# One fused kernel's feed-forward stage, reordered: the second product 14 slots behind the first, the token maximum between taps, VectorE's results in PSUM, the second norm's steps spread out

## What is computed

```
h  = layernorm(x1)
h  = bit_linear(h, w1)          # 1024 -> 4096: tokens rounded to 127 levels of their own maximum,
                                #               weights rounded to -1, 0, 1
h  = depthwise_conv1d(h)        # three taps along the sequence, one set for each of 4096 channels
h  = silu(h)
out = x1 + bit_linear(h, w2)    # 4096 -> 1024, tokens rounded to 127 levels of their own maximum
```

## Time and profile before

| what | value |
|---|---|
| runs | 1073.35 us median of three (1069.76 to 1102.9) |
| the profiled execution | 1075.98 us, of which the slowest core's span is 1074.4 us |
| spans of the 8 cores | 1056.5 to 1074.4 us |
| busy share of the span | PE 83%, DVE 75%, ACT 65%, POOL 64% |
| second stage | 522.1 us to the end, 552 us |
| first product of slots 0, 16, 24, 48, 56 begins | 522.1, 634.5, 698.2, 888.7, 947.7 us |
| the last first product ends | 1000.7 us |

### The profile page before, as it was taken

How to read it: one execution, slowest core, us unless ns; L and a number is a source line. 1 busy time by engine, 2 the same in 40 slices (tenths; PEclk the granted TensorE clock), 3 DMA queues, 4 the chain that set the end, 5 groups by cost and what they waited for, 6 DMA issues and landing times.

```text
span 1074.4 us, 23923 instructions; the slowest of 8 cores (1056.5 to 1074.4 us)
## 1 busy us (share of the span) xinstructions
PE 895.0 (83%) x7282; PEld 539.3 (50%) x7340; DVE 806.9 (75%) x1293; ACT 698.2 (65%) x1116; POOL 682.7 (64%) x912
## 2 busy tenths in 40 slices
PE   2999989897957778866676578999989899999898
PEld 1454545454524444433554455666656565666443
DVE  2674776777778888977377979898897989888631
ACT  3553888797827676868686866767677676766200
POOL 2211755646655768565454795959879597979590
PEclk9999999999979999967888989999999999999899
DMA  8910777666665766684744221423314233332112
GB/s 265 328 62 1 197 209 236 244 201 223 206 211 173 217 196 202 211 296 161 261 172 182 71 87 59 158 99 132 125 66 151 99 121 116 116 105 96 40 41 77
DMA packets 38749, 166.89 MB, mean 155 GB/s; under 512 B 4833, under 2 KB 4962, under 8 KB 29922
## 3 DMA queue, kind: packets, MB, share of 16 engines
q1 hardware_dynamic: 34210, 148.59, 41.8%
q0 software_dynamic: 4416, 16.78, 4.4%
HBM read 140.18 MB, written 25.17 MB: 154 GB/s over the span
## 4 chain that ended last, share of the span: by engine, by line
PE 42%; DVE 19%; issue 12%; POOL 9%; ACT 8%; DMA 7%; DVEq 1%; SPq 1%; POOLq 0%; ACTq 0%
PE psM L843 9%; PE psO L861 9%; POOL hs L618 6%; PE psQK L680 6%; PE psV L660 5%; PE psS L738 5%; PE psPV L757 5%; DVE hs L1367 3%; ACT PT L999 3%; DVE t1s L1208 3%; DVE amx L1386 3%; ACT hs L1044 2%; DMA wvst<-wv 2%; DMA t1scr<-t8s 2%; ACT tb L1048 2%
## 5 line engine op out<-in xcount | busy, mean ns | idle before, releaser
L999 ACT ACTIVATE PT<-psS,nbias 128x1024 bf16<-128x1024 f32 (+1 forms) x320 | 297.5, 985 | 89.2 <-PE psS L738 85.5
L843 PE MATMUL psM<-xqT,w1b 128*128 128x258 bf16 x2048 | 249.7, 283 | 44.3 <-DVE hs L1367 35.6
L609 POOL TENSOR_TENSOR hs<-hs,tb 128x256 f32<-128x256 f32 x256 | 200.1, 811 | 106.7 <-DVE hs L1367 106.1
L843 PEld LDWEIGHTS psM<-xqT,w1b 128*128 128x128 fp8e4 x2048 | 203.9, 101 | 91.5 <-issue 54.1
L1044 ACT ACTIVATE hs<-psM,convb_s,convw_s 128x256 f32<-128x256 f32 x256 | 146.3, 572 | 99.5 <-PE psM L843 88.0
L618 POOL TENSOR_TENSOR hs<-hs,srow 128x256 f32<-128x256 f32 x256 | 190.0, 775 | 12.0 <-ACT srow L1062 12.0
L680 PE MATMUL psQK<-ln1T,wqkb 128*128 128x512 bf16 x430 | 116.6, 391 | 23.3 <-DVE qkO L1135 7.4
L757 PE MATMUL psPV<-vaug,PT 128*128 128x65 bf16 x2176 | 116.9, 200 | 19.7 <-DVE ctx L1189 10.7
L757 PEld LDWEIGHTS psPV<-vaug,PT 128*128 128x128 bf16 x2176 | 93.1, 101 | 80.1 <-issue 59.4
L1367 DVE SCALAR_TENSOR_TENSOR hs<-psM,convw_s,hs 128x256 f32<-128x256 f32 x256 | 108.5, 473 | 20.1 <-ACT tb L1048 19.4
L1048 ACT ACTIVATE tb<-psM,convw_s 128x256 f32<-128x256 f32 x256 | 121.7, 475 | 0.0
(11 more groups left out here) (125 smaller groups left out, 1132.8 us busy)
## 6 DMA issues: line engine op xcount, KB each, us to landing
wbuf<-w1q SPq DMA_DIRECT2D x32, 1024.0 KB, 6.4
wbuf<-w2p SPq DMA_DIRECT2D x32, 1024.0 KB, 5.9
w1b<-t1scr SPq DMA_DIRECT2D x64, 512.0 KB, 3.5
x<-x SPq DMA_DIRECT2D x16, 512.0 KB, 15.0
wqkst<-wqk POOLq DMA_DIRECT2D x16, 512.0 KB, 6.7
x1scr<-x POOLq DMA_DIRECT2D x4, 2048.0 KB, 10.1
x1g<-x1scr SPq DMA_DIRECT2D x16, 512.0 KB, 4.4
out<-x1g SPq DMA_DIRECT2D x16, 512.0 KB, 2.6
```

The source lines that it names most:

```text
L609: e.tensor_tensor(hs_quad(q)[:, part], hs_quad(q)[:, part], tb_quad(q)[:, part], ALU.add).then_inc(g_add, 1)
L843: inst = e.matmul(psM[j][:, 0:GRP + 2], w1b[:, at:at + 128], xqT[:, x0:x0 + GRP + 2], start=(kc == 0), stop=(kc == 7))
L999: e.activation(out=pt_unit(u).rearrange("p (h w) -> p h w", w=512)[:, :, 128 * j:512], in_=psS[u % 2][:].rearrange("p (h w) -> p h w", w=512)[
```

## The change

Nothing changes in what is computed. The parts are:

1. **Lag.** The second product runs 14 slots behind the first (`LAG`), so it begins in slot 14 and ends in slot 77. Its eight parts come in another order: the first half of the channels for both output halves, then the second half for both. The tables are moved: quad 3 is scaled in b=3 instead of b=4, quad 7 in b=6 instead of b=7, quad 3 is rounded in b=4 instead of b=5 and quad 7 in b=7 instead of b=0 of the group after.
2. **Maximum between taps.** On DVE `widen_max(q-1)` stands between the taps of tiles 0 and 1 and those of tiles 2 and 3 of slot q; before, it stood behind all four. The rounding stands at the end of a slot.
3. **PSUM.** A bank `psD` holds `amx`, the identity that `token_scale` multiplies, and most of the small columns of the second norm. The bank comes from `psTb` and `psNb`, which now share one; for that `transpose_xq` and `turn_max` wait for each other's readers.
4. **Divided norm.** `stats` becomes `moments2`, `largest` and `smallest`, placed one at a time in slots b=4 to b=7 and b=0; before, both tiles' steps stood in b=0 and b=1. The batch for group 1 moves into the last pair of heads (steps 29, 31 and 36), and `x1t` has four slots. In group 0 rounding and transposes come two slots earlier.
5. **DMA.** The four loads of `w2T` are issued in slots 3 to 6, one each; before, all four in slot 5.

```
-        SCALED = {2: (0, 1), 3: (2,), 4: (3, 4), 5: (5,), 6: (6,), 7: (7,)}
-        ROUNDED = {3: (0, 1), 4: (2,), 5: (3, 4), 6: (5,), 7: (6,)}
+        SCALED = {2: (0, 1), 3: (2, 3), 4: (4,), 5: (5,), 6: (6, 7)}
+        ROUNDED = {3: (0, 1), 4: (2, 3), 5: (4,), 6: (5,), 7: (6, 7)}
+        LAG = 14
...
+        TAKEN = (1, 3)
...
-            def second(g, b):
-                m, n, half = b // 4, (b // 2) % 2, b % 2
+            def second(k):
+                g, i = divmod(k, 8)
+                m, half, n = i // 4, i // 2 % 2, i % 2
...
-                    if G >= 2:
-                        second(G - 2, b)
+                    if LAG <= 8 * G + b < LAG + 8 * NGRP:
+                        second(8 * G + b - LAG)
...
                     e.wait_ge(v_max, q)
-                    done(e.tensor_reduce(amx[:], rows, AX.X, ALU.max,
+                    done(e.tensor_reduce(psD[:, 0:GRP], rows, AX.X, ALU.max,
                                          apply_absolute_value=True))
                     settled()
-                    e.tensor_tensor(top, top, amx[:], ALU.max
+                    e.tensor_tensor(top, psD[:, 0:GRP], top, ALU.max
                                     ).then_inc(v_max, 1)
...
             for G in range(NGRP + 2):
                 for b in range(8):
                     if G < NGRP:
-                        taps(8 * G + b)
-                    if b == 0 and 2 <= G <= NGRP + 1:
-                        round_h(8 * (G - 2) + 7)
+                        taps(8 * G + b, (0, 1))
+                    if 1 <= 8 * G + b <= 8 * NGRP:
+                        widen_max(8 * G + b - 1)
+                    if G < NGRP:
+                        taps(8 * G + b, (2, 3))
+                    if b == 1 and 1 <= G <= NGRP:
+                        token_scale(G - 1)
+                    if 8 * G + b > LAG + 2 and (8 * G + b - LAG) % 4 in (0, 3):
+                        k = 8 * G + b - LAG - 1
+                        add_out(k // 4 * 2 + k % 2)
+                    if G < 6:
+                        if b == 4:
+                            moments2(G + 2, 0)
+                        if b == 5:
+                            largest(G + 2, 0)
...
                     if 1 <= G <= NGRP:
                         for k in ROUNDED.get(b, ()):
                             round_h(8 * (G - 1) + k)
```

More of the change, by code:

```diff
@@ L98, in build_program @@
         d_w1 = [sem("d_w1_0"), sem("d_w1_1"), sem("d_w1_2")]
-        d_x1t = [sem("d_x1t0"), sem("d_x1t1"), sem("d_x1t2")]
+        d_x1t = [sem(f"d_x1t{i}") for i in range(4)]
         d_x1g = [sem("d_x1g0"), sem("d_x1g1")]
@@ L303, in lcol, with pcol @@
             return lnc[:, at:at + n]
+        def pcol(i, k, n):
+            at = 384 + 48 * (i % 2) + 3 * k
+            return psD[:, at:at + n]
         def hs_quad(q):
@@ L408, in load_x1t, with load_w2 @@
             def load_x1t(st):
-                if st >= 8:
-                    e.wait_ge(a_xqf, st - 2)
-                e.dma_start(out=x1t[:, (st % 3) * D:(st % 3 + 1) * D],
+                if st >= 9:
+                    e.wait_ge(a_xqf, st - 3)
+                e.dma_start(out=x1t[:, (st % 4) * D:(st % 4 + 1) * D],
                             in_=x1scr[128 * st:128 * (st + 1), :]
-                            ).then_inc(d_x1t[st % 3], 16)
+                            ).then_inc(d_x1t[st % 4], 16)
+            def load_w2(q4):
+                if q4 == 0:
+                    e.wait_ge(a_xqf, 5)
+                e.dma_start(out=w2T[:, 8 * q4 * D:8 * (q4 + 1) * D],
+                            in_=t2scr[:, 8 * q4 * D:8 * (q4 + 1) * D]
+                            ).then_inc(d_w2, 16)
             def load_x1g(u):
@@ L429, in _ @@
             e.wait_ge(d_x1s[1], 16)
-            for st in (5, 6, 7):
+            e.wait_ge(d_x1s[2], 16)
+            for st in range(5, 9):
                 load_x1t(st)
@@ L1262, in var_of, with variance @@
                     "p (n k) -> p n k", k=2)[:, :, 1]
-            def spread(i):
+            def variance(i):
                 n = len(batch(i))
@@ L1345, in _ @@
                     place_bias(c - 1)
-                if hp == NP - 1 and s in (9, 12, 16):
-                    stats(0, s // 4 - 2)
-                if hp == NP - 1 and s == 16:
-                    spread(0)
-                if hp == NP - 1 and s == 21:
-                    factors(0)
+                if hp == NP - 1:
+                    if s in (12, 14, 17):
+                        moments2(0, (12, 14, 17).index(s))
+                        largest(0, (12, 14, 17).index(s))
+                        smallest(0, (12, 14, 17).index(s))
+                    if s == 17:
+                        variance(0)
+                    if s == 21:
+                        factors(0)
+                    if s in (29, 31):
+                        moments2(1, (s - 29) // 2)
+                        largest(1, (s - 29) // 2)
+                        smallest(1, (s - 29) // 2)
+                    if s == 31:
+                        variance(1)
+                    if s == 36:
+                        factors(1)
                 if slot in STEPS:
@@ L1360, in _, with taps @@
             attention_over(e)
-            def taps(q):
-                for j in range(4):
+            def taps(q, js):
+                for j in js:
                     hh = 4 * (q % 8) + j
@@ L1432, in add_out @@
                                        ALU.mult, ALU.add).then_inc(v_epi2, 1)
+            done(e.tensor_copy(psD[:, 256:384], idf[:]))
+            settled()
             for G in range(NGRP + 2):
@@ L1436, in _ @@
                     if G < NGRP:
-                        taps(8 * G + b)
-                    if b == 0 and 2 <= G <= NGRP + 1:
-                        round_h(8 * (G - 2) + 7)
+                        taps(8 * G + b, (0, 1))
[13 more added lines that the diff above has]
+                            largest(G + 2, 0)
+                        if b == 6:
+                            smallest(G + 2, 0)
+                        if b == 7 and G < 5:
+                            moments2(G + 2, 1)
+                    if 1 <= G < 7:
+                        if b == 0 and G < 6:
+                            largest(G + 1, 1)
+                        if b == 0 and G < 6:
+                            smallest(G + 1, 1)
+                        if b == 0:
+                            variance(G + 1)
+                        if b == 2:
+                            factors(G + 1)
                     if 1 <= G <= NGRP:
```

156 lines of the change are left out of this document (74 added, 82 removed).

## The result

| | before | after |
|---|---|---|
| median of the five runs | 1073.35 us | 1102.2 us (from 1097.66) |
| ratio | 1 | 1.024 (1.019 to 1.029) |
| profiled execution | 1075.98 us, span 1074.4 | 1097.66 us, span 1096.1 |

The change makes the kernel 2.4% slower (1.9 to 2.9). The forecast was 1074 us with a range up to 1091; it was wrong. Two of the five runs after (1128.02 and 1152.42 us) were in a slower state at a lower granted clock; ratios, and all times of runs from here on, are of the undisturbed runs, after 1099.7 us in the middle of three.

A forecast was written before the change was run, and what follows sets the result against it. DVE bounded middle groups before; afterwards POOL's chain plus the joint would. Group 0 +8.6 us, middle groups 61.4 against 63.5 and a shorter tail summed to 1075.4 against a 1074.4 span; forecast 1074 us, range 1048 to 1091.

The forecast's parts named there:

- The cycle: Silu, maximum, taps 2 and 3, PE and ACT's taps wait in a ring: 7.0 us a slot; group 0 +8.6 us.
- The middle group: One group with second product and norm: joint 20.9 plus POOL's chain 40.5, 61.4 us against 63.5.
- the joint: From the last add of one POOL chain to the start of the next, through silu, maximum, taps and PE: 20.9 us.
- GpSimd's chain: POOL's unbroken work from the end of the adds of b=2 to those of b=7: 40.5 us.
- With a second product that is PE's own 7.0 and costs nothing.: Slots with a second product: the new 7.0 us wait cycle equals PE's own slot time, so no cost.
- VectorE no longer the bound: DVE's own bound of 63.5 us a group is gone; it then needs about 53 us.
- additions at 0.43 us: Seven DVE additions in each group fall from 0.77 to some 0.43 us with PSUM, -2.4 us.
- Two half sums hidden in slots 14 and 15: POOL's chain already takes longer than PE there, so two half sums, 6.9 us, cost nothing.
- Tail -3.45: At the end six half sums instead of seven remain behind the last rounding: -3.45 us.
- The Trainium skill's rule on PSUM sources: VectorE pays fixed 120 cycles with a PSUM source, 58 with SBUF; would make the sum some 4 us higher, 1078.
- PE becomes the bound: Faster rival: joint 3 us shorter, no clock cost in group 0; groups 58.4 us, total 1049; chance 0.17.
- The attention's end moves: Rival: rounding of the last weights stands behind the moved batch on DVE, +2 to +5 us, 1078; chance 0.08.

The follow-up runs named there:

- b1_max_between: Kernel before with one edit: the maximum of the slot before stands between VectorE's taps of tiles 1 and 2; 1121.8 us, ratio 1.044.
- e3_before_two_behind: Kernel before with split taps and, between them, the maximum of the quad two slots back; 1079.3 us, ratio 1.007.

## Why the prediction was wrong

*The cycle.* The mechanism was right: 7.0 us for a slot from rows, 7.03 measured. Group 0 to the end of slot 8's first product (583.79 + 1.92 = 585.7, from 519.10) took 66.6 us against 64.0 forecast, inside the bounds. GpSimd's first scaling stands 88.6 us behind the stage's start (607.72), forecast 87.1. So group 0 added 1.5 us to the error. That it is free of waits for `w1b` was right for this core; six of the others wait 2.0 to 3.4 us in slot 3, and the wait in the old order is above.

*The middle group* is the term that failed: 61.4 us forecast, 65.3 in the group shown. The larger share is *the joint*, 20.9 forecast and 23.6 measured. The prediction lets the first product of b=1 end 6.0 us behind the last add, through silu, maximum, tap and PE alone. It ended 8.4 behind it. The prediction has no term for the rounding of quad 7: that rounding stands in b=7 at the end of the slot, and with the maximum ahead of it PE's half sum in b=0 waits for it, 2.25 us idle, and 5.30 instead of 3.45 for the half sum, 4.1 us. With the rounding moved ahead the groups take 63.1 us and the joint 21.4, near the forecast 20.9.

*GpSimd's chain* was forecast at 40.5 us and is 41.7. It took 6 additions at 0.35 us off for contention that would go; single additions of GpSimd still take 1.17 us where the others take 0.73, and before, the chain with one quad less takes 40.2 in a middle group, not the 39.5 that group 7 with two `place_xqs` would give.

Five scalings are 65.0 us apart on the mean (607.72 to 932.91) against 61.4 forecast: 18.2 us, of which about 10 lie in the joints and 8 in the chains; 1.6 of the 8 are the stall of the last section. With 1.5 for group 0, -3.0 for the start and 4.0 for what follows 932.91 this is the 20.7 us between 1075.4 and the span of 1096.1. The other 7 us up to the median of 1102.2 lie between this execution, the shortest of the five, and the median; this trace can't tell them.

*"With a second product that is PE's own 7.0 and costs nothing."* This sentence hid the price. It holds for a slot in the steady state. It doesn't for the joint, where GpSimd's next chain hangs on the sequence of steps and each wait for silu is added to it: 23.6 against 16.3 us in the run without that wait. The prediction itself wrote that in the old order the adds of b=2 come 3 us sooner, and did not ask what the kernel would be with that alone. The loss was set against gains of the other parts, and the sum came out near zero; by the runs the order loses 56 us and the other parts gain 30.

*VectorE no longer the bound; additions at 0.43 us; small steps at 0.2*: right (0.425 us; 0.15 to 0.21 with one of 0.7). *DVE needs 53 us*: 52.4. Without the PSUM bank the run is 17 us longer, without the divided norm 23.

*Two half sums hidden in slots 14 and 15*: right by the run with a lag of 16. *Tail -3.45*: it fell by 4.3 us, for reasons of which the forecast had one. Six half sums stand behind the last rounding instead of seven, as counted, but they end 22.7 us behind it, against 24.5 before, so that gives 1.8; in the kernel with the old order of VectorE they take 21.0, the whole 3.4. The other 2.6 us lie between the last turn and the first scaling, 5.0 us instead of 7.6, which the forecast kept "as now": the half sum between the two takes 6.02 us before and 3.62 after. That the number came out near is in part luck.

*The Trainium skill's rule on PSUM sources* that was weighed ("VectorE: DVE Perf Modes") was left out of the sum, and the additions bear that out (0.425 us; the last section has one instruction that agrees with the rule).

*Rivals.* The slower side was given 0.12, for contention of GpSimd with VectorE. The time came out at that rival's 1099, above its 64.5 us a group, but contention is at most the 1.2 us of the chain; removing the wait for silu takes 7.3 us off the group and leaves the chain as it is. "PE becomes the bound", 58.4 us a group, is what the kernel does without the wait: 58.0, with PE busy for 57.5. "The attention's end moves" did not happen on this core (-3.0 us); on the mean of the eight cores the stage starts 3.3 us later, of which some is scatter, as b1_max_between and e3_before_two_behind, whose first stage is that of the kernel before, start 1.4 and 2.1 us later too.

## What to carry to other kernels

Work of an in-order queue that waits for another engine's answer to the previous step must not stand ahead of the work that gives that engine its next step. Either place it last or let it take the result of two steps ago; here the second costs a changed index and a special case for the last quad of a group, and is worth 57 us. A cycle that equals the bound of a steady slot is not free: add it up at the joints between groups, where the next chain waits for it. And when a step is pushed back in a queue, list every engine that waits for it (here PE, in the slot after) before it is called free.
